# Sixteen slots of a fused decoder layer dealt anew: scans, row maxima, projections and statistics change places

## The reference

```python
# 1: gated linear attention, 16 heads, key width 8, value width 16
log_gate = log_sigmoid(x @ Wg1 @ Wg2) / 16
state = state * exp(log_gate)[..., None] + k[..., :, None] * v[..., None, :]   # over the 512 tokens
o     = einsum('bhd,bhde->bhe', q, state)
x = layernorm(x + (silu(x @ Wg + bg) * normalised(o)) @ Wo)
# 2: cross attention to ctx, 16 heads of width 16
attn = softmax(Q @ K.T / sqrt(16))
x = layernorm(x + (attn @ V) @ W_o + b_o)
# 3: mix with the previous token, r = sigmoid(xr @ W_r.T), k = relu(xk @ W_k.T)**2
x = layernorm(x + r * (k @ W_v.T))
```

## Time and profile before

| | us |
|---|---|
| three runs | 661.21, 669.42, 669.73 |
| median | 669.42 |
| the profiled execution | 668.88 |
| its span, first to last instruction | 667.1 |
| busy: PE / DVE / ACT / POOL | 483.8 / 409.8 / 293.0 / 202.9 |

### The profile page before, as it was taken

How to read it: one execution, slowest core, us unless ns; L and a number is a source line. 1 busy time by engine, 2 the same in 40 slices (tenths; PEclk the granted TensorE clock), 3 DMA queues, 4 the chain that set the end, 5 groups by cost and what they waited for, 6 DMA issues and landing times. The chain is left out here.

```text
span 667.1 us, 6036 instructions
## 1 busy us (share of the span) xinstructions
PE 483.8 (73%) x1844; PEld 198.1 (30%) x1844; DVE 409.8 (61%) x636; ACT 293.0 (44%) x498; POOL 202.9 (30%) x201
## 2 busy tenths in 40 slices
PE   3522846459978686999787967798988778896662
PEld 1200332004332121354432313444223333231441
DVE  3289167863476789436877988467655557523224
ACT  1320523205556254545484637153856325855031
POOL 0058449722224556411235564112000010000000
PEclk9855888559999688999895969897969889976766
DMA  4880384601623520260255102001311100000000
GB/s 139 260 218 0 95 224 139 161 14 35 156 88 88 172 80 1 80 157 18 87 124 121 49 1 80 32 32 40 102 52 32 63 1 1 1 2 23 10 0 31
DMA packets 36608, 50.21 MB, mean 75 GB/s; under 512 B 5952, under 2 KB 29152, under 8 KB 36576
## 3 DMA queue, kind: packets, MB, share of 16 engines
q1 hardware_dynamic: 33456, 41.23, 21.6%
q10 hardware_dynamic: 3120, 8.59, 5.0%
HBM read 39.12 MB, written 10.49 MB: 74 GB/s over the span
## 5 line engine op out<-in xcount | busy, mean ns | idle before, releaser
L963 DVE TENSOR_REDUCE MX<-bank 128x1 f32<-128x512 f32 x256 | 169.5, 682 | 142.9 <-PE bank L462 142.2
L766 ACT ACTIVATE PT<-bank 128x512 f32<-128x512 f32 x256 | 146.1, 595 | 171.4 <-PE bank L471 163.3
L462 PE MATMUL bank<-KS,QS 96*128 96x512 bf16 x256 | 106.9, 427 | 59.1 <-DVE MX L963 42.8
L471 PE MATMUL bank<-QS,KS 99*128 99x512 bf16 x256 | 105.7, 423 | 21.2 <-ACT PT L766 13.5
L1033 POOL TENSOR_TENSOR W<-qT,W 128x512 f32<-128x512 f32 x64 | 88.1, 1378 | 99.8 <-DVE W L874 99.2
L874 DVE TENSOR_TENSOR_SCAN W<-bank,W 128x512 f32<-128x512 f32 x64 | 77.6, 1215 | 8.2 <-POOL W L1022 7.5
L485 PE MATMUL bank<-PT,Vs 128*32 128x512 f32 x512 | 80.4, 705 | 0.8 <-ACT PT L766 0.8
L462 PEld LDWEIGHTS bank<-KS,QS 96*128 96x128 bf16 x256 | 25.8, 102 | 121.6 <-DVE MX L963 75.9
L471 PEld LDWEIGHTS bank<-QS,KS 99*128 99x128 bf16 x256 | 25.1, 101 | 120.5 <-issue 66.0
L1068 POOL TENSOR_TENSOR MP<-MX,zero 128x16 bf16<-128x16 f32 x16 | 4.8, 300 | 153.5 <-DVE MX L963 81.1
L869 DVE TENSOR_TENSOR W<-kT,W 128x512 f32<-128x512 f32 x40 | 37.9, 948 | 12.2 <-DMA W<-v_rows 12.1
(11 more groups left out here) (118 smaller groups left out, 617.0 us busy)
## 6 DMA issues: line engine op xcount, KB each, us to landing
W<-v_rows SPq DMA_DIRECT2D x16, 512.0 KB, 8.4
W<-v_rows ACTq DMA_DIRECT2D x16, 512.0 KB, 7.9
KS<-k_parts SPq DMA_DIRECT2D x96, 64.0 KB, 2.3
QS<-q_parts SPq DMA_DIRECT2D x96, 64.0 KB, 2.3
k_parts<-parts SPq DMA_DIRECT2D x12, 256.0 KB, 2.1
q_parts<-parts SPq DMA_DIRECT2D x12, 256.0 KB, 4.5
xT<-in_xT SPq DMA_DIRECT2D x4, 512.0 KB, 3.9
cT<-in_cT SPq DMA_DIRECT2D x4, 512.0 KB, 3.5
```

Source lines behind the costliest of these rows:

```text
L462: pe.matmul(bank(n)[:, :], QS[0:NS, h, i * P:(i + 1) * P], KS[0:NS, h, :], start=True, stop=True).then_inc(filled(n), 1)
L471: pe.matmul(bank(name)[:, :], KS[0:NR, h, kt * P:(kt + 1) * P], QS[0:NR, h, :], start=True, stop=True).then_inc(filled(name), 1)
L766: act.activation(PT[:, n % 2, j, :], bank(name)[:, :], ACT.Exp).then_inc(emptied(name), 1)
L963: dve.tensor_reduce(MX[:, NT * h + i:NT * h + i + 1], bank(n)[:, :], AX.X, ALU.max).then_inc(emptied(n), 1)
```

## The change

The sets of instructions stay the same: each engine still runs the same operations on the same tiles. What changes is the place, and with it some banks and waits.

```diff
-LAG = 5
+LAG = 6
 SIDE_USES = {
-    (1, 0): ("gv0", "r", 2), (1, 1): ("gv1", "r", 0), (1, 2): ("var", "o", 1), (1, 3): ("gg", "r", 2),
-    (2, 0): ("y0", "f", 0), (2, 1): ("y1", "f", 1),
-    (3, 0): ("gq", "r", 1), (3, 1): ("gk", "r", 0), (3, 2): ("K0", "o", 2), (3, 3): ("K1", "o", 1),
...
+    (0, 0): ("V0", "b", 2), (0, 1): ("V1", "b", 1), (1, 2): ("K0", "o", 2), (1, 3): ("K1", "o", 1),
+    (2, 0): ("var", "o", 0), (2, 2): ("y0", "f", 2), (3, 0): ("y1", "f", 1), (3, 2): ("gv0", "r", 0),
+    (4, 0): ("gy0", "o", 2), (4, 1): ("gy1", "o", 1), (4, 2): ("gv1", "r", 0),
+    (5, 0): ("gg", "r", 2), (5, 1): ("gq", "r", 0), (5, 2): ("gk", "r", 1), (5, 3): ("t0", "f", 2),
...
 def decay_slot(s):
-    return (5, 1) if s < 0 else (7, 3)
+    return (6, 3) if s < 0 else (7, 0)
+def scan_quarter(s, e):
+    return 27 + 3 * e // 2 if s == -1 else 29 + 34 * e // 15
+SCANS = {s: {scan_quarter(s, e): e for e in range(DV)} for s in STEPS}
+SUM_QUARTERS = {s: {(35, 41, 47, 54)[q] if s == -1 else (40, 48, 57, 66)[q]: q for q in range(RQ)} for s in STEPS}
-for _which, _slot, _quarters, _heads in (("b", 0, 10 * NT, range(LAG, H)), ("o", 10, 5 * NT, range(LAG))):
+for _which, _slot, _tiles_in, _heads in (("b", 0, (4, 5, 6, 5, 6, 2, 5, 2, 3, 2), range(LAG, H)),
+                                         ("o", 10, (2, 4, 4, 4, 5, 5), range(LAG))):
-PARTS = {(2, 3): ("b", 1), (6, 2): ("b", 2), (10, 1): ("b", 3), (14, 0): ("o", 0)}
-ROWS = {(3, 2): ("b", 1), (6, 3): ("b", 2), (10, 3): ("b", 3), (14, 3): ("o", 0)}
+PARTS = {(2, 1): ("b", 1), (5, 1): ("b", 2), (10, 1): ("b", 3), (14, 2): ("o", 0)}
+ROWS = {(2, 3): ("b", 1), (5, 3): ("b", 2), (10, 3): ("b", 3), (15, 0): ("o", 0)}
@@ SP: the keys' parts and keys_in(o, 0) now stand ahead of the values @@
+                if o is not None:
+                    for p, part in enumerate((K_hi, K_mid, K_lo)):
+                        ...
+                    keys_in(o, 0)
                 if r is not None:
                     sp.wait_ge(v_32, count(ND, r, ND))
@@ ACT @@
-                if at in ((1, 2), (1, 3)):
-                    m = at[1] - 2
+                if at in ((3, 3), (4, 3)):
+                    m = at[0] - 3
                     act.wait_ge(*full_of(f"gv{m}", r))
-                if (slot, at[1]) in ((0, 1), (1, 1)):
+                if at in (((5, 3), (6, 3)) if s < 0 else ((7, 2), (9, 2))):
                     act.wait_ge(v_out, count(16, r, 16))
-                if at == (4, 0):
+                if at == (2, 0):
                     for m in range(ND):
                         act.wait_ge(*full_of(f"K{m}", o))
@@ DVE @@
-            def statistics(n, src, b):
-                for tt in range(NT):
+            def statistics(n, src, b, half):
+                for tt in (2 * half, 2 * half + 1):
-                if at == (0, 1):
+                if at == (13, 2):
                     dve.wait_ge(z_ln, ...)
@@ POOL @@
+                e = SCANS[s].get(quarter + 4)
+                if e is not None and r > 0 and e % 2 == 0:
                     pool.tensor_tensor(W[:, e, :], kT[:, :], W[:, e, :], ALU.mult).then_inc(u_pool, 1)
-                if at == (1, 0):
+                if at == (14, 3):
                     pool.wait_ge(z_sig, ...)
                     pool.tensor_tensor(kz[:, 1:3, :], kz[:, 1:3, :], ab[:, 1:3, :], ALU.mult).then_inc(gate_z, 1)
```

314 lines of the change are left out of this document (156 added, 158 removed), and 8 rows, old and new, of the table SIDE_USES.

## The result

| | us |
|---|---|
| before: median of 4 runs (lowest, highest) | 666.26 (661.21, 669.73) |
| after: median of 4 runs (lowest, highest) | 636.63 (635.48, 640.37) |
| ratio, 95% interval | 0.957 (0.948 to 0.966) |
| profiled execution after, and its span | 635.70, 633.9 |
| mean granted clock before, after | 0.827, 0.879 |

The change makes the kernel 4.3% faster.

The account below looks back on a forecast made before the run. No engine is full; a step takes nearly the sum over slots of the fullest engine's work, as shared banks couple PE, DVE and ACT. 668.9 - 17 (levelling) - 5 (queries) + 2 (step -1) = 649 us, range 638 to 668.

Parts of the forecast that it names:

- Levelling, -17: Steps 0 to 3: evening out engine work between slots takes 16.9 us off the tally, ends -8 and -18.
- the tally: Sum over slots of the fullest engine's priced work; steps 0 to 3 go from 405.3 to 388.4 us.
- levelling worth little: First rival: engines are coupled by the quarter, not the slot, so levelling gives only -8; 663 us, chance 0.28.
- The third step, "doesn't gain": Step 3: no scans and no o stage, slots already short, so no gain; 95 to 97 us.
- The clock, taken at nothing in the sum: Steps 0 to 3: the 54 us of slow clock and hand-overs above the tally stay as they are.
- a rival (639 us): Third rival, the clock case: fewer uneven slots raise PE's clock, perhaps 10 us over four steps; chance 0.1.
- Waits for the queries, -5: Slot 10 of steps 0 and 1: PE's waits of 3.8 and 3.1 us shrink; -5, ends 0 and -6.9.
- Step -1, +2: Step -1: later transfers into `W`, faster scans, more maxima before the row; +2 us, ends -3 and +9.
- My 18 to 20 us from the end of step -2's sums: Step -1: chain over batch 0's gate, gy and gv1 until the transfers into `W`, where it was 8 us.
- values come late: Second rival: values land late, scans start a slot late in steps 0 and 1, step -1 +13; 679 us, chance 0.1.
- my sign for steps 0 and 1: Steps 0 and 1: DVE never waits for transfers into `W`.
- DVE in slot 5 at 6 to 7 us: Sign of levelling: DVE's work in slot 5, 10.5 us in step 1 before, falls to 6 to 7 us.

Follow-up runs that it names:

- the five parts taken back singly: Changed kernel with maxima, scans, three projections, statistics or the gate's sigmoid each put back as before: 638.28, 640.17, 653.73, 638.03, 635.32 us.
- the doubled scores: Every score tile of slots 8 to 15 multiplied twice into the same bank: 668.76 us on the kernel before, 643.28 on the changed kernel.
- the kernel with early values: Changed kernel with step -1's values projected in slot 1 and stored from `ka` ahead of the keys: 635.47 us.
- with PE's waits filled: Changed kernel plus constant matmuls before PE's sums in steps -2, -1 and the last batch's projections: 632.29 us; with the gate as before too, 627.96.

## Why the prediction was right, and where it was wrong

**Levelling, -17: its size isn't shown.** I had step 0, 1, 2 at 111, 124 and 107 us and found 111.2, 123.5 and 101.4. The first two fit, but not for my reason alone: they also hold the 3.8 and 3.1 us of the queries' waits, and 8 and 17 us less at 1.2 GHz, which I had at nothing. Steps 0 and 1 fell by 15.7 us together; less the queries that is 8.8 for levelling and clock, where the tally alone has 12.9. DVE's and ACT's waits for PE fell (30 and 43 us), but a faster PE shortens them too, and PE's own waits for DVE's maxima did not fall (39.8, then 42.8). Levelling may have kept them from growing while PE became faster; no kernel here separates that. The tally was of use for the single parts: nothing for the maxima (without them it is 3.5 shorter, measured 2 longer, within the noise), little for the scans (+1.6, measured 4), 5.7 for the projections in steps 0 and 1 (measured 6 to 8). But the five parts taken back singly come to 1.9 of its 17 us (-3.5, +1.6, +5.7, +1.1, -3.0). The rest lies in moves that no kernel takes back alone, K0, K1, `var`, gv0, gv1, y0, y1, gy and the pieces of stage f, among them t0 by seven quarters and r0 by nine, or in moves that act only together. So the rival "levelling worth little" is not ruled out: its time, 663, is far off, but the gain over it can be the clock's.

**The third step, "doesn't gain": wrong.** I had it at 95 to 97 us and it took 88.6. The tally is unchanged for it (78.2 and 78.9), so by this reckoning nothing of the 7.1 is levelling. PE's idle time in it is 17.4 us both times; what fell is its busy time, from 78.3 to 71.2. The time at 1.2 GHz in it fell from 26.2 to 10.2 us. In kernels whose step 3 has the changed kernel's instructions in the changed kernel's places, it takes 88.5 to 88.9 us with 10.2 at the lower clock, and 91.3 or 91.4 with 17.1 (the kernels with the scans, the projections or the gate undone, which stages that step 3 doesn't hold). That is 0.4 us for each microsecond at 1.2 GHz; 16 times 0.4 is 6.4, which leaves 0.7 for all else.

**The clock, taken at nothing in the sum: the step that failed.** I let the 54 us between tally and steps, slow clock among them, "stand as they are", and priced the rise as a rival (639 us) at -10 with a chance of 0.1. That rival is what happened, and by more. The estimate of 97 us of PE's work in step 1 from which it was made stands in no row; the earlier trace rows has 111 busy. In steps 0 to 3 the time at 1.2 GHz fell from 104 to 43 us, and PE's busy time by 23.9. The two fit: at 1.2 GHz half of each busy microsecond is lost (3.62 against 1.88 above), PE is busy for some 83% of these steps, and 61 times 0.5 times 0.83 is 25. That is about the most the clock can have given there, since a faster matmul ahead of a pause that another engine sets only makes the pause longer.

A lower estimate comes from repeated runs of one and the same kernel (the kernel before 36 times, the others 4 to 10 times each): the time is longer by 0.27 us for each microsecond at 1.2 GHz. The time at 1.2 GHz fell by 68, so -18 us. This price is rough. It is a correlation, the time itself stands on both sides of it, and within single kernels it runs from 0.04 to 0.48.

Why the clock rose is not settled. I had thought that the slots heavy on DVE, in which PE paused, are gone; the sum of those waits says otherwise. What did fall in steps 0 to 3 is the number of PE's waits over 1 us, from 28 with 51.5 us in all to 20 with 31.6, the two for the queries among them. No kernel holds the places and changes the clock alone; the doubled scores, which change it with the places fixed, are the nearest thing.

**The sum, term by term.** Tally -17, queries -7, later start +4, clock -18 make -38; the spans differ by 33.2 and the medians by 29.6 to 33. So these terms overlap by 5 to 8 us, or one of them is too large. By PE's own account of steps 0 to 3 it is busy time -23.9, the queries' waits -6.9 and all other waits -3.7, which would leave the tally little beside the clock. I can't part them further.

**Waits for the queries, -5: the waits right, their price not shown.** Both are gone whole, 6.9 us, which was the end of my range. But they are gone as well in the kernel before with the new maxima, which is not faster, and in the changed kernel with the maxima dealt as before. In the first, other slots lost again what this had won. So -7 is what was waited, not what was shown to be won. That slots 9 and 10 lost 15.0 us together was not in it: about 2 are the tally's, and the matmuls behind each wait no longer run at 1.2 GHz.

**Step -1, +2 (measured +3.8): right within 2, by errors that cancel, which is luck.** I had the transfers into `W` at 90 and the first scan at 97; they came at 94.8 and 102.5. My 18 to 20 us from the end of step -2's sums were 21.1 (73.7 to 94.8), so the chain was right; its beginning was 4.3 us late. I had costed step -2 at nothing, and there POOL's gate product had moved ahead of the last query products. The keys' issues ahead of the store in SP's list, nine of them with 8.9 us, were also costed at nothing, and that held within 1: they end at 91.8, ACT's copy of the values at 91.0. The scans then took 38 us and not 41, and from the last scan's end to the first exponential it was 13.7 us. Before it had been 11.2 (139.2 to 150.4), so that the row of maxima behind 13 tiles instead of 9 cost 2.5 and not 3.5. The rival **values come late** thus happened in its cause (POOL waited 13.3 us for `W` in three places, the longest 9.2, in step -1) but not in its price: DVE waited 4.9 us in all for these transfers, where it had waited 12.1, and all of it in step -2, so that my sign for steps 0 and 1 held (POOL waited once there, 3.3 us in step 0); and in step -1 the chain over the gate and the decay ended at the same time, as the kernel with early values shows.

**DVE in slot 5 at 6 to 7 us: wrong.** In step 1 it was busy for 8.0 us of slot 5, with 9.1 before. Norms and residual additions of the slots beside it seem to fall into it, which I haven't followed instruction by instruction. The tally does not hold slot by slot: it has 8.6, 8.4 and 7.4 us for slots 2, 4 and 7 of step 1, which are 12.6, 9.1 and 10.6 us long, and 6.7 for slot 6, which is 3.9.

**The range.** It ended at 638 with the words that it leaves out "a little of the clock case"; the clock case happened, and a range with room for it would have held the result. The row of slots of step 1 now adds up to 116.4 as printed, not 116.2, which changes nothing. With half of the 18 us taken into the sum the forecast would have been 640.

## What to carry to other kernels

Where engines hand tiles over through a few banks, add up the fullest engine slot by slot; the difference between two such sums gave the right direction here, and told that one part, the maxima, is worth nothing; its size as a whole was not confirmed. But read the granted clock beside it: a change that takes out long pauses of TensorE can also take out time at 1.2 GHz, and steps that the tally leaves alone gain too. Set PE's busy time before and after beside its idle time: that tells which of the two has fallen. The first steps of a pipeline are chains and not loads: follow them from the step before, with what each moved instruction is put ahead of on every engine, and look for a second chain that ends at the same time.

## What the runs showed of the hardware

- A microsecond at the lower clock goes with 0.27 us in this kernel (0.29 within the 36 runs of the kernel before, 0.28 within four of the changed one and 0.48 within its other four), with 0.3 in the end after step 3 and 0.4 in step 3. It isn't a fixed price: with PE's waits filled the granted clock rose from 0.88 to 0.91 to 0.92, some 50 us less at 1.2 GHz, for 4 us of time, because most of those microseconds had been waits.
- Repeated runs of one program differ in PE's granted clock (0.867 to 0.879 for the changed kernel), and the time goes with it in part (640.37 at 0.867, 635.48 at 0.879, but also 639.03 at 0.877 and 633.46 at 0.876).
- The clock fell in step 3 of the changed kernel, twice and for 10.2 us in all, though no wait of PE there was longer than 1.90 us; the first time during that wait.
- A DVE product with two SBUF inputs took 2.79 us beside a POOL product of 2.34, as against 0.67 just before; scans and maxima, which read a bank, kept their time beside the same product.
- 128 further matmuls in the kernel before, 28 us of PE's time, cost nothing in the median (668.76 against 668.92): steps 0 to 3 became 7.0 us longer and the end 4.6 shorter in the profiled executions.
